# A graph network of four message-passing layers: dense layer, scores and heads projected in other lots, with two buffers

## The reference

```python
edge_index = jnp.stack([src, dst])
x = _layernorm(x + _L0_gnn_ref(x, edge_index, edge_weight, L0_gnn_W, L0_gnn_b), axis=-1)
x = _layernorm(x + _L1_gnn_ref(x, edge_index, L1_gnn_w, L1_gnn_fc_w, L1_gnn_fc_b, L1_gnn_bias), axis=-1)
x = _layernorm(x + _L2_gnn_ref(x, edge_index), axis=-1)
x = _layernorm(x + _L3_gnn_ref(x, edge_weight, edge_attr_3, edge_index, ...), axis=-1)
```

```python
# L0: weighted sum over incoming edges, then a dense layer
agg = jax.ops.segment_sum(norm[:, None] * x[edge_index[0]], edge_index[1], num_segments=x.shape[0])
return jax.nn.relu(agg @ W + b)                      # W is 32 x 32
# L1: graph attention with 4 heads
hp = jnp.einsum('nf,hfo->hno', h, w)                 # w is 4 x 32 x 32
a_src = jnp.einsum('hnf,f->hn', hp, w_src)
a_dst = jnp.einsum('hnf,f->hn', hp, w_dst)
e = jax.nn.leaky_relu(a_src[:, src] + a_dst[:, dst] + fc_b[0], negative_slope=0.2)
att = softmax of e over the edges of each src        # segment_max, exp, segment_sum
agg = jax.vmap(lambda m: jax.ops.segment_sum(m, src, num_segments=n))(att[:, :, None] * hp[:, dst, :])
return agg.mean(axis=0) + bias
```

## Time and profile before

| | |
|---|---|
| median of 3 runs | 27719.22 us |
| lowest and highest | 27716.97 and 27924.35 us |
| the profiled execution, its own time | 27758.51 us |
| its span | 27756.8 us |
| busy: POOL | 16913.9 us (61%) |
| busy: PE | 13056.3 us (47%) |
| busy: DVE | 11400.3 us (41%) |
| busy: ACT | 5617.9 us (20%) |
| DMA | 794.43 MB, mean 29 GB/s |

### The profile page before, as it was taken

The page is one execution under the profiler, slowest core; times in us unless marked ns, Lnnn a source line. Parts: engine busy times, 40 slices in busy tenths (PEclk is TensorE's granted clock), DMA queues, the critical chain, the costliest instruction groups (busy, mean ns, idle before and its releaser), DMA issues. The chain is left out here.

```text
span 27756.8 us, 312901 instructions
## 1 busy us (share of the span) xinstructions
PE 13056.3 (47%) x63827; PEld 12457.6 (45%) x63828; DVE 11400.3 (41%) x24717; ACT 5617.9 (20%) x17566; POOL 16913.9 (61%) x16986
## 2 busy tenths in 40 slices
PE   0333333333333338997333333333333368888887
PEld 0233322333333338996333333333333357777777
DVE  2377711111111117775111111111111179999999
ACT  6422221100000002221000000000000035555554
POOL 1677766456666660001666666666666668888887
PEclk8555555555555558887555555555555578888888
DMA  1111111222222221110000000200000022222223
GB/s 47 14 15 15 15 14 14 12 54 58 58 59 58 58 58 29 30 30 21 12 11 12 12 11 11 13 12 12 12 11 11 11 36 43 43 43 43 43 43 41
DMA packets 2490687, 794.43 MB, mean 29 GB/s; under 512 B 1958608, under 2 KB 2281393, under 8 KB 2489651
## 3 DMA queue, kind: packets, MB, share of 16 engines
q0 software_dynamic: 517120, 331.99, 8.9%
q1 hardware_dynamic: 1623714, 242.33, 5.3%
q10 hardware_dynamic: 349748, 219.11, 3.1%
HBM read 699.49 MB, written 93.71 MB: 29 GB/s over the span
## 5 line engine op out<-in xcount | busy, mean ns | idle before, releaser
L990 POOL DMA_INDIRECT hop_far<-hop_rows,hop_index x6464 | 6113.6, 946 | 5816.4 <-issue 4739.0
L1026 PE MATMUL hop_total<-hop_far,hop_hot 128*128 128x32 f32 x12928 | 3019.3, 378 | 6228.5 <-issue 3426.9
L1026 PEld LDWEIGHTS hop_total<-hop_far,hop_hot 128*128 128x128 f32 x12928 | 2973.7, 323 | 6275.5 <-issue 6274.1
L773 POOL DMA_INDIRECT weighted_far<-in_x_dram,weighted_rows x3232 | 3342.4, 1034 | 1973.1 <-issue 1031.2
L1005 DVE TENSOR_TENSOR hop_hot<-hop_iota,local_of_edge 128x512 f32<-128x512 f32 x1616 | 1057.9, 687 | 8119.2 <-DMA rows_by_src<-push_row,push_index 6369.5
L1098 POOL DMA_INDIRECT rows_by_src<-push_row,push_index x3232 | 3103.9, 960 | 1705.3 <-issue 1586.4
L2123 POOL DMA_INDIRECT conv_far<-conv_rows x3232 | 3322.2, 1028 | 964.6 <-issue 865.1
L1148 PE MATMUL push_near<-far_rows_sb,push_turned 128*128 x6464 | 1636.0, 434 | 3166.8 <-issue 2344.3
L857 PE MATMUL weighted_total<-weighted_message,weighted_hot 128*128 128x33 f32 x6464 | 1514.6, 404 | 3345.6 <-issue 2050.8
L2229 PE MATMUL conv_radial_a<-radial,conv_hidden 128*128 128x256 f32 x6464 | 2737.5, 511 | 640.7 <-DVE conv_products_b L2361 564.9
L1148 PEld LDWEIGHTS push_near<-far_rows_sb,push_turned 128*128 128x128 f32 x6464 | 1553.4, 328 | 3249.4 <-issue 3247.8
(11 more groups left out here) (256 smaller groups left out, 20609.0 us busy)
## 6 DMA issues: line engine op xcount, KB each, us to landing
push_line<-local_by_group ACTq DMA_DIRECT2D x808, 256.0 KB
hop_far<-hop_rows,hop_index POOLq DMA_INDIRECT x6464
conv_weights<-weight_by_group SPq DMA_DIRECT2D x808, 128.0 KB
att_far<-rows_by_src SPq DMA_DIRECT2D x880, 80.0 KB
weighted_far<-in_x_dram,weighted_rows POOLq DMA_INDIRECT x3232
push_place<-place_by_dst SPq DMA_DIRECT2D x3232, 0.5 KB
rows_by_src<-push_row,push_index POOLq DMA_INDIRECT x3232
conv_rows<-edges_by_dst SPq DMA_DIRECT2D x3232, 4.0 KB
```

The source lines that it names most:

```text
L773: pool.indirect_dma_start(far[s][:, j, :], None, table, bass.IndirectOffsetOnAxis(ap=rows[s][:, j, 0:1].bitcast(I32), axis=0)).then_inc(ga ...
L990: pool.indirect_dma_start(far[s][:, j, :], None, table, bass.IndirectOffsetOnAxis(ap=index[s][:, j:j + 1], axis=0)).then_inc(gathered[s], 16)
L1026: last = pe.matmul(total[:].rearrange("p n c -> p (n c)")[:, bass.ds(at[s % SLOTS * HALVES + j // COLUMNS] * F, F)], hot[s][:, j, :], far[ ...
```

## The change

Dense and scores move to a new function, project_quads. It takes 14 bins at a time (LOT), 7 lots in all, and treats four neighbouring bins of 32 features (QUAD) as one operand with 128 rows: one transpose turns the four, and one matmul multiplies them with a weight matrix of 128 rows that holds the 32-row weights four times on its diagonal and zeros elsewhere. The last group of a lot has two bins. Its buffers turned, turned_ps and out are doubled; PE transposes lot n+1 before it multiplies lot n. Dense packs all sums in one copy first, and its finish has two steps instead of three; scores are transposed straight from x. All loops over batches or lots are unrolled.

Heads stay in project_parts with 7 bins a batch; staged, turned, turned_ps and out are doubled there, VectorE stages batch n+1 before it waits for batch n, and PE transposes n+1 before it multiplies n.

Setup clears w0 and scorer and loads w0 into its four diagonal blocks and w1_by_f into four quadrants, each by a DMA of its own; the scorer's sums are reduced once for each quadrant.

```diff
 BATCH = 7
+LOT = 14
+QUAD = P // F
 MUL = 8
 RANGE = 50.0
...
+        blank = k.sem("weights_blank")
...
+            dve.memset(k.w0[:], 0.0).then_inc(blank, 1)
+            dve.memset(k.scorer[:], 0.0).then_inc(blank, 1)
...
-            sp.dma_start(k.w0[:], k.in_w0).then_inc(loaded, 16)
+            sp.wait_ge(blank, 2)
+            for q in range(QUAD):
+                own = slice(q * F, (q + 1) * F)
+                sp.dma_start(k.w0[own, own], k.in_w0).then_inc(loaded, 16)
+                sp.dma_start(k.w1_by_f[own], k.in_w1.rearrange("h f o -> f h o")).then_inc(loaded, 16)
             sp.dma_start(k.b0[:], k.in_b0.partition_broadcast(P)).then_inc(loaded, 16)
             sp.dma_start(k.w1[:], k.in_w1.rearrange("h f o -> (h f) o")).then_inc(loaded, 16)
-            sp.dma_start(k.w1_by_f[:], k.in_w1.rearrange("h f o -> f h o")).then_inc(loaded, 16)
-            sp.dma_start(k.fc[:], k.in_fc[0, :].partition_broadcast(F)).then_inc(loaded, 16)
+            sp.dma_start(k.fc[:], k.in_fc[0, :].partition_broadcast(P)).then_inc(loaded, 16)
...
-def project_parts(nc, k, ctx, name, source, depth, weights, width, finish):
+def project_memory(nc, ctx, name):
+    return [[ctx.enter_context(nc.psum_tensor(f"{name}_{n}{c}", [P, width], F32)) for c in range(2)]
+            for n, width in (("turned_ps", 8 * P), ("out", 512))]
+def project_parts(nc, k, ctx, name, memory, source, depth, weights, width, finish):
+    BATCHES = BINS // BATCH
     def sem(n):
         return k.sem(f"{name}_{n}")
-    staged = ctx.enter_context(nc.sbuf_tensor(f"{name}_staged", [P, BATCH, depth], F32))
-    turned = ctx.enter_context(nc.sbuf_tensor(f"{name}_turned", [depth, BATCH, P], F32))
-    turned_ps = ctx.enter_context(nc.psum_tensor(f"{name}_turned_ps", [P, 8 * P], F32))
-    out = ctx.enter_context(nc.psum_tensor(f"{name}_out", [P, 512], F32))
+    staged = [ctx.enter_context(nc.sbuf_tensor(f"{name}_staged{c}", [P, BATCH, depth], F32)) for c in range(2)]
+    turned = [ctx.enter_context(nc.sbuf_tensor(f"{name}_turned{c}", [depth, BATCH, P], F32)) for c in range(2)]
+    turned_ps, out = memory
     rows_staged, rows_turned, copied, multiplied = sem("rows_staged"), sem("rows_turned"), sem("copied"), sem("multiplied")
     own = sem("steps")
     def vector(dve):
         s = Steps(dve, own)
-        with loop(dve, 0, BINS // BATCH) as i:
-            s.restart()
-            source(dve, s, i, staged)
+        def stage_rows(n):
+            source(dve, s, n, staged[n % 2])
             s.wait()
             dve.sem_inc(rows_staged, 1)
-            dve.wait_ge(multiplied, i + 1)
-            finish(dve, s, i, out[:, 0:BATCH * width].rearrange("p (b w) -> p b w", b=BATCH))
+        stage_rows(0)
+        for n in range(BATCHES):
+            if n + 1 < BATCHES:
+                stage_rows(n + 1)
+            dve.wait_ge(multiplied, n + 1)
+            finish(dve, s, n, out[n % 2][:, 0:BATCH * width].rearrange("p (b w) -> p b w", b=BATCH))
             s.wait()
     def tensor(pe):
-        with loop(pe, 0, BINS // BATCH) as i:
-            pe.wait_ge(rows_staged, i + 1)
+        def turn_rows(n):
+            pe.wait_ge(rows_staged, n + 1)
             for b in range(BATCH):
-                last = pe.transpose(turned_ps[0:depth, b * P:(b + 1) * P], staged[:, b, :], k.ident[:])
+                last = pe.transpose(turned_ps[n % 2][0:depth, b * P:(b + 1) * P], staged[n % 2][:, b, :], k.ident[:])
             last.then_inc(rows_turned, 1)
-            pe.wait_ge(copied, i + 1)
+        turn_rows(0)
+        for n in range(BATCHES):
+            if n + 1 < BATCHES:
+                turn_rows(n + 1)
+            pe.wait_ge(copied, n + 1)
             for b in range(BATCH):
-                last = pe.matmul(out[:, b * width:(b + 1) * width], turned[:, b, :], weights,
+                last = pe.matmul(out[n % 2][:, b * width:(b + 1) * width], turned[n % 2][:, b, :], weights,
                                  start=True, stop=True)
             last.then_inc(multiplied, 1)
     def scalar(act):
-        with loop(act, 0, BINS // BATCH) as i:
-            act.wait_ge(rows_turned, i + 1)
-            act.copy(turned[:].rearrange("f b p -> f (b p)"),
-                     turned_ps[0:depth, 0:BATCH * P]).then_inc(copied, 1)
+        for n in range(BATCHES):
+            act.wait_ge(rows_turned, n + 1)
+            act.copy(turned[n % 2][:].rearrange("f b p -> f (b p)"),
+                     turned_ps[n % 2][0:depth, 0:BATCH * P]).then_inc(copied, 1)
     return vector, tensor, scalar
-def project(nc, k, *what):
+def quad_memory(nc, ctx, name):
+    return [[ctx.enter_context(nc.psum_tensor(f"{name}_{n}{c}", [P, 512], F32)) for c in range(2)]
+            for n in ("turned_ps", "out")]
+def project_quads(nc, k, ctx, name, memory, rows, weights, width, finish, stage_rows=None):
+    LOTS = BINS // LOT
+    def sem(n):
+        return k.sem(f"{name}_{n}")
+    turned = [ctx.enter_context(nc.sbuf_tensor(f"{name}_turned{c}", [P, 512], F32)) for c in range(2)]
+    turned_ps, out = memory
+    rows_ready, rows_turned, copied, multiplied, finished = (
+        sem(n) for n in ("rows_ready", "rows_turned", "copied", "multiplied", "finished"))
+    own = sem("steps")
+    quads = [(q * P, q * QUAD, min(QUAD, LOT - q * QUAD)) for q in range(-(-LOT // QUAD))]
+    def vector(dve):
+        s = Steps(dve, own)
+        if stage_rows:
+            stage_rows(dve, s)
+            s.wait()
+        dve.sem_inc(rows_ready, 1)
+        for n in range(LOTS):
+            dve.wait_ge(multiplied, n + 1)
+            finish(dve, s, n, out[n % 2][:, 0:LOT * width].rearrange("p (b w) -> p b w", b=LOT))
+            s.wait()
+            dve.sem_inc(finished, 1)
+    def tensor(pe):
+        def turn_rows(n):
+            for at, first, bins in quads:
+                last = pe.transpose(turned_ps[n % 2][0:bins * F, at:at + P],
+                                    rows[:, n * LOT + first:n * LOT + first + bins, :].rearrange("p b f -> p (b f)"),
+                                    k.ident[:])
+            last.then_inc(rows_turned, 1)
+        pe.wait_ge(rows_ready, 1)
+        turn_rows(0)
+        for n in range(LOTS):
+            if n + 1 < LOTS:
+                turn_rows(n + 1)
+            pe.wait_ge(copied, 2 * n + 2)
+            if n >= 2:
+                pe.wait_ge(finished, n - 1)
+            for at, first, bins in quads:
+                last = pe.matmul(out[n % 2][:, first * width:(first + bins) * width],
+                                 turned[n % 2][0:bins * F, at:at + P], weights[0:bins * F, 0:bins * width],
+                                 start=True, stop=True)
+            last.then_inc(multiplied, 1)
+    def scalar(act):
+        for n in range(LOTS):
+            act.wait_ge(rows_turned, n + 1)
+            whole, _, bins = quads[-1]
+            act.copy(turned[n % 2][:, 0:whole], turned_ps[n % 2][:, 0:whole]).then_inc(copied, 1)
+            act.copy(turned[n % 2][0:bins * F, whole:whole + P],
+                     turned_ps[n % 2][0:bins * F, whole:whole + P]).then_inc(copied, 1)
+    return vector, tensor, scalar
...
+    packed = ctx.enter_context(nc.sbuf_tensor("packed_sums", [P, BINS, F], F32))
+    def pack_sums(dve, s):
+        s.step(dve.tensor_copy(packed[:], sums[:, :, 0:F]))
+    def finish(dve, s, n, out):
+        x = k.x[:, n * LOT:(n + 1) * LOT, :]
+        s.step(dve.tensor_tensor(k.update[:], out, spread(k.b0[:], 1, LOT), ALU.add))
         s.wait()
-        s.step(dve.tensor_scalar(k.update[:], k.update[:], 0.0, None, ALU.max))
-        s.wait()
-        s.step(dve.tensor_tensor(x, x, k.update[:], ALU.add))
-    dense = project_parts(nc, k, ctx, "dense", source, F, k.w0[:], F, finish)
+        s.step(dve.scalar_tensor_tensor(x, k.update[:], 0.0, x, ALU.max, ALU.add))
+    memory = quad_memory(nc, ctx, "first")
+    dense = project_quads(nc, k, ctx, "dense", memory, packed, k.w0[:], F, finish, pack_sums)
...
+            for q in range(QUAD):
+                own = slice(q * F, (q + 1) * F)
+                at = (2 * q + half) * HEADS
+                s.step(dve.tensor_reduce(k.scorer[own, at:at + HEADS], k.scorer_parts[own], AX.X, ALU.add))
...
+    def scores_finish(dve, s, n, out):
+        lot = slice(n * LOT, (n + 1) * LOT)
+        s.step(dve.tensor_scalar(k.own_score[:, lot, :], out[:, :, 0:HEADS], k.fcb[:], None, ALU.add))
+        s.step(dve.tensor_copy(k.far_rows[:, lot, F + 1:F + 1 + HEADS], out[:, :, HEADS:2 * HEADS]))
+    scores = project_quads(nc, k, ctx, "scores", memory, k.x, k.scorer[:], 2 * HEADS, scores_finish)
...
+        k.w0, k.b0 = sb("w0", [P, QUAD * F]), sb("b0", [P, F])
+        k.w1, k.w1_by_f = sb("w1", [HEADS * F, F]), sb("w1_by_f", [P, HEADS, F])
...
+        k.update = sb("update", [P, LOT, F])
```

More of the change, by code:

```diff
@@ L1234, in project @@
+def project(nc, k, name, *what):
     with stage(nc, k) as ctx:
-        vector, tensor, scalar = project_parts(nc, k, ctx, *what)
```

(5 more changed lines are left out.)

24 lines of the change are left out of this document (3 added, 21 removed).

## The result

The changed kernel took 27673.0 us (median of 17 executions, 27484.0 to 27722.6), the kernel before 27896.8 (17 executions, 27717.0 to 27930.9). The ratio is 0.9924 with a 95% interval of 0.9903 to 0.9945: 0.8% faster, within 1%.

The account below looks back on a forecast made before the run. Three dense, scores and heads projections, 351 us together, were taken as serial chains with one engine working at a time. 99 + 92 + 26 - 1.3 - 2.8 = 213 us off 27719.2 gave 27506 us, range 27440 to 27630.

Parts of the forecast that it names:

- dense: Dense projection, copy of the sums to last update: 119.0 to 19.8 us, 99 saved, with the clock rising after 5.0.
- scores: Scores projection, from the memset on: 104.7 to 13.1 us, 92 saved (84 at the low clock), with staging gone.
- scorer: Scorer's weights reduced for four quadrants: 6 more reductions of at most 0.2 us, 1.3 us lost.
- heads and way in: Heads: period 8.15 us instead of 9.63, 22.6 less, plus the loop's 3.5 in the way in; 26 us saved.
- setup: Setup: six more weight DMAs on SyncE's queue, ahead of the sort's first load; 2.8 us more, exposed.
- Off the median: 27506 us: Whole kernel: the 213 us gain taken off 27719.2, the median of the runs, 0.77% less.
- 12.3 with the clock rising after 5.0 us: Scores: TensorE's 19.5 us at the lower clock shrink to 12.3 because the clock rises after 5.0 us.
- the 19.5 us of my own rival: Scores: seven lots of 2.78 us with the clock staying low; no separate chance, inside the forecast's 0.70.
- The low clock: Rival for dense and scores: clock stays at 0.50, 8.8 + 7.3 us less gain, 27522; within the forecast's 0.70.
- Heads at the upper level: Rival for heads: 5.0 us of unbroken TensorE work raises the clock, about 31 us more gain, 27475; chance 0.12.
- Instruction supply: Rival for the unrolled heads: new code costs 3.5 us a piece, taking back 20 us, 27526; chance 0.05.
- the move of the tiles: Placement rival: tiles shifted 1376 bytes slow gathers and scatters; 13 ns each cancels the gain; chance 0.06.

Follow-up runs that it names:

- e12: The kernel before, unchanged, profiled once more on the slower sort of chip; its span is 27883.3 us.
- e4: The kernel before plus an unused tile of 1376 bytes a partition; group medians 25271.9 and 25456.4 us against 25277.6 and 25459.4.
- e9: The kernel before, unchanged, profiled again on a chip of the quicker sort; its span is 25443.2 us.
- e5: The changed kernel, run again without edits; group medians 27532.1 and 27686.4 us against 27738.9 and 27922.1 for the kernel before.
- e6: The changed kernel with each bin's 8 scorer columns padded by 24 zero columns; group medians 27519.7 and 27688.7 us, scores 15.0 instead of 20.1.
- e11: The changed kernel with the padded scorer of e6 and the heads' staging of e7; 0.9874 of the kernel before, 25008.6 and 25202.2 us.
- e7: The changed kernel with heads staged two batches ahead; groups at 27473 and 27646 us, heads 65.8 us instead of 103.1.
- e10: The kernel before with its three projection loops unrolled and nothing else; ratio 0.9999 over all executions, 39 us less upper with upper.
- e2: The kernel before with only the heads made double-buffered and unrolled; groups 41 and 45 us lower, heads 103.0 us.
- e3: The kernel before with all three projections double-buffered at 7 bins, no block-diagonal weights; groups 96 and 108 us lower.
- e8: The changed kernel with each lot transposed only after the previous lot's matmuls; dense 33.0 us, scores 27.4 us.

## Why the prediction was right and wrong

Term by term, against the changed kernel's profile and, where the stages of before are needed, the rows named in the prediction:

| term | predicted | measured |
|---|---|---|
| dense | 119.0 to 19.8, 99 less | 18.9, 100.1 less |
| scores | 104.7 to 13.1, 92 less | 20.0, 84.7 less |
| scorer | 1.3 more | 22.3 to 24.1, 1.8 more |
| heads and way in | 26 less | 141.2 to 106.4, 34.8 less |
| setup | 2.8 more | 19.76 to 22.69, 2.9 more |
| sum | 213 less | 214.9 less |
| whole span, e12 to changed | | 213.6 less |

That the sum is right to 2 us is in part luck: scores gave 7 us less than predicted and heads 9 more.

**The step that failed** is the base: "Off the median: 27506 us". The 213 us were close, but I took them off 27719.2, a median of three. Of three executions two were 2 us apart and the third 205 above them; I read it as "some of the difference between runs", when it was a second level, as likely as the first. In 17 executions the median is 27896.8, on that second level and 178 us higher, which is the whole miss: 27506 and 178, less the 11 us by which the medians part more than 213, is 27673. The range ended at 27630. From rows that stood there, it could have been drawn to 27924 - 213 = 27711. What makes the level is the attention stage and its clock (0.98 or 0.89, e4 with e9; e5 with e6), which the change does not touch; why the clock differs there stays open. That the profile's own span, 27757, lay near the lower level hid it: it was slow attention and quick gathers together.

**Dense** came out 1 us under its sum, with two terms off: the packing copy took 1.79 us, not 3.4, since I scaled it at 1.04 ns an element from a copy of 7 bins and from one of 2970 elements whose source lies in PSUM; the way in took 1.36 and not 1.1; PE's stream, 5425.43 to 5439.57, was 14.1, against 13.9. The 0.285 a pass held (2.27 / 8). The Trainium skill, VectorE: DVE Perf Modes, section "What auto-detection actually checks", says that a single-source copy with source and result in SBUF doubles its rate only if the outermost non-unit dimensions are both even or equal. The rows (0.39 for 224 elements, 1.79 for 3136, which is 0.57 ns each) agree if the packed result counts as one run: 7 against 224 is neither both even nor equal, 98 against 3136 is both even. Counted by bins on both sides, 7 and 7 are equal, and the short copy should have been quick too. No run changes only that.

**Scores** failed on one term: "12.3 with the clock rising after 5.0 us". The clock did not rise, and the 19.5 us of my own rival came true. I had carried the rise over from the zero matmuls, whose passes move 512 columns; e6 and e11 show it with 128, and scores move 32. The Trainium skill, TensorE: Matmul & The Clock Gate, section "What's actually happening", has activity release the gate; by busy time alone scores (19.32 of 20 us) should have risen, so here the measurement decides, and unbroken work was not enough. Nor do the rows give a rule in its place: the heads, whose multiply moves 32 columns, ran at the upper level for a few us in e6 and e11 and not in the others.

**Heads** were right in mechanism (one chain, confirmed by e7) and 9 us too dear. A period was 7.47, not 8.15: finish 0.85 with its hand-over, since the loop's bookkeeping left that place too (0.97 before), staging 1.88 instead of 1.98, one hand-over of 0.12, and transposes and matmuls 4.59 instead of 1.76 + 3.19, because the matmuls start 1.55 after the transposes and overlap their end once the wait for the copy is gone. Twelve periods of 0.68 are 8 us. The way in lost 3.1, not 3.5.

**Rivals.** The low clock came in scores and not in dense. Heads at the upper level did not come: 0.50 for 102 us, with 4.6 us of unbroken work in each batch. Instruction supply is out (e10: no hole in the unrolled loops), and so is the move of the tiles (e4). Within 1% was right.

## What to carry to other kernels

A second buffer gives overlap only if every engine's order lets it: write out, for each engine, what stands between one batch's wait and the next batch's start, and move the staging ahead of the wait (37 us here for a few lines). Where small matmuls are paid by the pass, pack them into one with block-diagonal weights, and watch the clock: wider passes with zeros can be quicker than narrow ones (15.0 against 20.1 us in e6). Before a gain under 1% is put as a time, look at the single executions for levels, and compare level with level.

## What the hardware showed that I had not expected

- TensorE busy 19.3 of 20 us (scores) and 61.8 of 66 us (e7) with 32-column passes between 128-column transposes stayed at 0.50; with 128-column passes it rose within 6 us (dense, e6).
- The clock of the same instructions differs between executions. In the heads' first batches it was at 1.00 for about 3 us in e6 and 7 in e11, and at 0.50 throughout in the changed kernel, e2, e3, e5, e7 and e8. e6 and e11 are executions of the lower group, the others of the upper. A gain of a few us at the upper level is not to be counted on.
- The same attention stage runs at a mean clock of 0.98 or 0.89, 2271 or 2441 us, in executions of one kernel, and so makes two levels of the whole.
- Chips differ in the gathers, or something that goes with the chip does: idle time of GpSimd in the push was 1777.4 us in e12 (chip 0) and 995.0 in e9 (chip 2), and the spans of the kernel before were 27,883 and 25,443 us. The group of e9:

```profile
L1098 POOL DMA_INDIRECT rows_by_src<-push_row,push_index x3232 | 3104.5, 961 | 995.0 <-issue 984.0 <-ACT push_row L1181 11.0
```
